# A transformer block on eight cores: the K and V projections of an attention stage moved into its layer-norm loop

## What is computed

```python
def _L1_attn_ref(x, wq, bq, wk, bk, wv, bv, wo, bo):
    q = jnp.einsum('bsd,hde->bhse', x, wq) + bq
    k = jnp.einsum('bsd,hde->bhse', x, wk) + bk
    v = jnp.einsum('bsd,hde->bhse', x, wv) + bv
    scale = 1.0 / jnp.sqrt(jnp.asarray(q.shape[-1], q.dtype))
    scores = jax.nn.softmax(jnp.einsum('bhse,bhte->bhst', q, k) * scale, axis=-1)
    att = jnp.einsum('bhst,bhte->bhse', scores, v)
    b, h, s, e = att.shape
    att = att.transpose(0, 2, 1, 3).reshape(b, s, h * e)
    return att @ wo.T + bo
```

## Time and profile before

| | us |
|---|---|
| median of the two runs | 11593.65 |
| lowest, highest | 11357.42, 11829.88 |
| the profiled execution | 11357.42 |
| its span on the slowest core | 11355.9 |
| spans of the eight cores | 11331.6 to 11355.9 |

### The profile page before, as it was taken

One profiled execution on the slowest core, in us unless ns is written; L12 is line 12 of the kernel. 1 busy time (PEld: TensorE's weight loads), 2 busy tenths in 40 slices (PEclk: granted clock), 3 DMA queues, 4 the chain that ended last, 5 costly groups with the idle time before them and its releaser, 6 DMA issues.

```text
span 11355.9 us, 101042 instructions; the slowest of 8 cores (11331.6 to 11355.9 us)
## 1 busy us (share of the span) xinstructions
PE 6804.2 (60%) x28548; PEld 2633.3 (23%) x28548; DVE 3976.3 (35%) x10242; ACT 3012.2 (27%) x6372; POOL 254.0 (2%) x410
## 2 busy tenths in 40 slices
PE   3344325545777748888833443255457777488888
PEld 2122111112222213333311221121122222133333
DVE  2443452233222232333424434522332222333334
ACT  1111123422555520111111111234225555201111
POOL 1000000001000000000000000000010000000000
PEclk7566557666888869999965665576668888699999
DMA  3000100003000011212220001000030000112121
GB/s 61 1 1 1 12 2 1 1 0 23 8 1 1 1 16 29 38 30 37 39 68 1 1 1 10 3 1 1 0 23 8 1 1 1 18 27 38 30 38 45
DMA packets 228448, 174.16 MB, mean 15 GB/s; under 512 B 137158, under 2 KB 188360, under 8 KB 227916
## 3 DMA queue, kind: packets, MB, share of 16 engines
q0 software_dynamic: 218688, 134.11, 9.0%
q1 hardware_dynamic: 9228, 33.58, 0.9%
HBM read 284.99 MB, written 16.78 MB: 27 GB/s over the span
## 4 chain that ended last, share of the span: by engine, by line
PE 46%; DVE 25%; ACT 12%; issue 11%; DMA 4%; DVEq 1%; SPq 0%; ACTq 0%; another core or an unknown queue 0%; POOL 0%; POOLq 0%
PE PS L1087 8%; PE PS L1100 5%; ACT AR L576 5%; PE PS L586 5%; DVE AR L601 4%; DVE AR L878 3%; DVE AR L1107 3%; PE PS L1040 2%; PE PS L1460 2%; PE PS L1019 2%; PE PS L844 2%; PE PS L1025 2%; PE PS L417 2%; DMA AR<-w2t 1%; PE PS L1484 1%
## 5 line engine op out<-in xcount | busy, mean ns | idle before, releaser
L576 ACT ACTIVATE AR<-PS 128x512 bf16<-128x512 f32 x2048 | 1119.3, 595 | 1166.6 <-PE PS L552 1002.1
L1107 DVE SCALAR_TENSOR_TENSOR AR<-PS,AR 128x512 f32<-128x512 f32 x1024 | 768.4, 751 | 1392.3 <-PE PS L1100 1335.4
L1087 PE MATMUL PS<-AR 128*128 128x512 bf16 x4096 | 944.1, 389 | 185.7 <-DMA AR<-w2t 185.7
L1100 PE MATMUL PS<-AR 128*128 128x512 bf16 x4096 | 988.0, 378 | 81.8 <-ACT AR L1092 25.4
L586 PE MATMUL PS<-AR 128*65 128x512 bf16 x2048 | 844.4, 428 | 202.3 <-ACT AR L576 191.6
L601 DVE RECIPROCAL AR<-PS 64x512 bf16<-64x512 f32 x128 | 428.8, 3350 | 1461.5 <-PE PS L596 1461.5
L417 PE MATMUL PS<-AR 128*128 128x128 bf16 x1024 | 210.5, 267 | 1059.3 <-DVE AR L412 925.7
L1092 ACT ACTIVATE AR<-PS 128x512 bf16<-128x512 f32 x512 | 305.8, 597 | 1859.5 <-PE PS L1087 1853.9
L1087 PEld LDWEIGHTS PS<-AR 128*128 128x128 bf16 x4096 | 404.3, 99 | 707.2 <-issue 243.7
L834 ACT ACTIVATE AR<-PS 128x512 bf16<-128x512 f32 x1024 | 523.1, 596 | 46.0 <-PE PS L812 45.2
L1100 PEld LDWEIGHTS PS<-AR 128*128 128x128 bf16 x4096 | 344.9, 96 | 704.3 <-issue 435.5
(11 more groups left out here) (229 smaller groups left out, 8285.1 us busy)
## 6 DMA issues: line engine op xcount, KB each, us to landing
AR<-w1t POOLq DMA_DIRECT2D x32, 1024.0 KB, 8.9
AR<-w2t POOLq DMA_DIRECT2D x32, 1024.0 KB, 8.8
AR<-x SPq DMA_DIRECT2D x32, 512.0 KB
y<-AR SPq DMA_DIRECT2D x32, 512.0 KB
AR<-sfc1t POOLq DMA_DIRECT2D x8, 1024.0 KB, 10.3
AR<-sfc2t POOLq DMA_DIRECT2D x8, 1024.0 KB, 15.4
AR<-sfc3t POOLq DMA_DIRECT2D x8, 1024.0 KB, 11.6
AR<-L_attn_Wq POOLq DMA_DIRECT2D x16, 256.0 KB, 13.3
```

The lines of the kernel that those rows point to most:

```text
L576: r.op("scalar", lambda s, ps=ps, pt=pt: s.activation(pt[:, 0:NIQ], ps[:, 0:NIQ], AF.Exp, bias=0.0, scale=0.125), reads=[ps.K], writes=[pt.K])
L1087: r.op("tensor", lambda t, e=e, tb=tb, hc=hc, c=c, PHx=PHx, w1T=w1T: t.matmul(PHx[:, 0:512], w1T[:, c * 512 + hc * 128: c * 512 + (hc + 1) ...
L1100: r.op("tensor", lambda t, tt=tt, dh=dh, hc=hc, PMx=PMx, hw=hw, w2T=w2T: t.matmul(PMx[:, 0:512], hw[:, hc * 512 + tt * 128: hc * 512 + tt ...
L1107: r.op("vector", lambda v, i=i, e=e, dh=dh, PMx=PMx: v.scalar_tensor_tensor(moeacc[:, i * D + dh * 512: i * D + dh * 512 + 512], PMx[:, 0: ...
```

## The change

Three edits. The two scratch tiles of the layer norm become one, in all stages. In L1 attention the call of the layer norm moves from the start of the stage to a place behind the weight issues and the bias loads. And the K and V projections become a callback of it: after each row tile's norm come the two halves of V for that tile, and after every fourth tile all eight K groups of that block of 512 rows. The V matmuls now name only the columns of `ufm` that they read. The number of matmuls, evictions and loads is the same. Since the norm now allocates behind the weights, its scratch lies above `bv_row`, in the bytes that the bias loads use for their row.

```diff
@@ emit_ln_ufm
     stats = ctx.sb(8 * nt, F32)
-    sq = [ctx.sb(D, F32), ctx.sb(D, F32)]
+    _sq = ctx.sb(D, F32)
+    sq = [_sq, _sq]
     utm = [ctx.sb(D, BF16), ctx.sb(D, BF16)]
@@ emit_l1_attn
     ufm = ctx.sb(nd * T, BF16)
-    emit_ln_ufm(ctx, R, ufm, T, D)
 
     kfm = [ctx.sb(T, BF16) for _ in range(npair)]
...
     pk = [ctx.pbank(0), ctx.pbank(1)]
-    for p in range(npair):
-        for icol in range(T // 512):
-            pp = pk[icol % 2]
...
-    for i in range(nt):
+
+    def kv_tile(i):
         for half in range(2):
             pp = pk[half % 2]
...
                     start=False, stop=(c == nd - 1)),
-                    reads=[ufm.K, wv_sb.K], writes=[pp.K])
+                    reads=[ufm.k(c * T + i * 128, c * T + (i + 1) * 128), wv_sb.K], writes=[pp.K])
...
+        if i % 4 == 3:
+            icol = i // 4
+            for p in range(npair):
+                pp = pk[p % 2]
+                for c in range(nd):
+                    r.op("tensor", lambda t, p=p, icol=icol, c=c, pp=pp: t.matmul(
+                        pp[:, 0:512], warn[p][:, c * 128:(c + 1) * 128],
+                        ufm[:, c * T + icol * 512: c * T + icol * 512 + 512],
+                        start=(c == 0), stop=(c == nd - 1)),
+                        reads=[warn[p].K, ufm.K], writes=[pp.K])
+                r.op("vector", lambda v, p=p, icol=icol, pp=pp: v.tensor_scalar(
+                    kfm[p][:, icol * 512:(icol + 1) * 512], pp[:, 0:512],
+                    bk_cols[:, p:p + 1], None, ALU.add),
+                    reads=[pp.K, bk_cols.k(p, p + 1)], writes=[kfm[p].k(icol * 512, (icol + 1) * 512)])
+
+    emit_ln_ufm(ctx, R, ufm, T, D, tile_cb=kv_tile)
     A.release()
```

## The result

| | before | after |
|---|---|---|
| median of all runs, us | 11658.27 (12 runs) | 11718.84 (13 runs) |
| lowest run, us | 11357.42 | 11531.80 |
| profiled execution, us | 11357.42 | 11543.04 |

The ratio of after to before is 1.0131, with a 95% interval of 1.0069 to 1.0193: slower, by less than the 2% that was called measurable. The profiled execution of after took 11543.0 us where 11538 was forecast. The median of all runs is 11718.84, outside the stated range of 11468 to 11595.

A forecast was written before the change was run, and what follows sets the result against it. A latency-bound norm precedes PE-bound K and V; the change makes the first V wait for loads. Stage delays of +93.9 and +86.5, together +180.4, on 11357.4 give 11538 us, 1.6% slower; range 11468 to 11595.

The forecast's parts named there:

- the wait for the loads and its queue: First V matmul waits for bo's landing, later transposes queued behind it on PE; PE idle 96 us in the first sequence.
- the chain behind V's second eviction: Next tile's small DVE operations follow V's second eviction; 5.97 us between V bursts, hiding only 2 of the norm's 7.9.
- the clock of V: Each V burst starts at 1.2 GHz and rises to 2.4 GHz within it, taking 6.2 us.
- the parts costed at nothing: One scratch tile instead of two, in all four stages, and the bf16 tiles moving down 4 KB: cost 0.
- The wq loads: Before the first Q matmul, three loads stay hidden under the last K: cost 0, else up to 4 us a sequence.
- Rival A: V stays at 1.2 GHz in all bursts, 7.69 us each: 48 us more, 11586 us, over 2% slower; chance 0.12.
- What the prediction took from Part 4 of that page: Transposes do not count as clock activity in the same way; the norm's 0.50 clock was said to agree.
- The 4.3 us at the low level: Time at 1.2 GHz within a V burst, taken as the middle of 5.5 and 2.9 us: 10 matmuls at 0.427.
- Rival B: V runs at 2.4 GHz throughout, 4.30 us a burst: 60 us less, 11477 us; chance 0.08.
- Rival C: No stall, since the weight loads start well before 2598 and land in time: 11353 us, or 11293; chance 0.05.
- D: The load chain's own length changes from 115 and 105 us: +9 or -9 us; no separate chance given.
- the base of the sum: Predicted delay added to the profiled execution, 11357.4 us, rather than the median 11593.65 of two runs 472 us apart.

The follow-up runs named there:

- e2: Changed kernel with the V/K callback for tile i called after the norm of tile i+12; ratio to before 1.0127, lowest run 11493.2 us, stage 264.8 us.
- e8: The kernel of e2 repeated in more rounds; ratio to before 1.0021, lowest run 11345.8 us, stage 265.0 and 263.5 us.
- e3: Changed kernel with wk and wv loads batched side by side; ratio to before 1.0061, lowest run 11439.8 us, stage 300.0 and 295.1 us.
- e4: Kernel before the change with the same batched wk and wv loads; ratio to before 1.0047, lowest run 11363.0 us, stage 264.7 and 263.9 us.
- e5: Changed kernel with the norm cut in two, next tile's front part ahead of V; lowest run 11601.4 us, no ratio, stage 301.2 and 304.0 us (core 5).
- e6: Changed kernel with unread matmuls added, 14 behind each V burst and three between transposes; lowest of four runs 11646.2 us, stage 322.9 us in one sequence.
- e9: The kernel of e6 repeated; ratio to before 1.0078, lowest of ten runs 11459.8 us, stage 320.7 and 318.5 us.
- e1: Kernel before with only the norm moved and one scratch tile, K and V in old order; ratio to before 0.9997, lowest run 11362.4 us.
- e7: Changed kernel with batched loads, norm cut in two and callback four tiles later; ratio to before 0.9925, lowest run 11299.1 us, stage 226.7 and 226.2 us.

## Why the prediction was right or wrong, point by point

| term, sequence 1 | forecast | after |
|---|---|---|
| tile 0 transposed at | 2617 | 2616.9 |
| idle time of PE at the first V | 96 | 92.1 |
| memset to first V | 114.7 | 111.5 |
| V burst, mean of 16 | 6.2 | 6.4 (5.6 to 7.2) |
| gap between V bursts | 5.97 | 5.6 to 6.1 |
| K, eight groups | 13.8 | 13.8 |
| first V to first Q | 244.0 | 246.7 |
| stage longer than before | +93.9 | +93.4 |

In the second sequence the first V came 108.2 us after the memset (105.5 forecast) and the first Q 247.5 later; the stage is 355.7 us, 92.7 more than before (86.5 forecast). Together +186.1 of the 185.6 by which the span grew, 11541.5 against 11355.9, so everything outside the stage stayed as it was. That the first sequence came within 0.5 us is partly luck: its load chain was 3.2 us shorter than forecast, and what follows 2.7 longer.

The mechanism is shown by the runs: the wait for the loads and its queue (e2, e8, e3, with e4 as the control), the chain behind V's second eviction (e5, less the part that is clock), the clock of V (e6, e9), and the parts costed at nothing (e1). The wq loads stayed hidden, as costed: the three that the first Q matmul needs were issued as below, while the last K groups ran until 2955.92, and the Q matmuls started at 2955.76 with no wait.

```profile
2944.38 0.93 POOL L477 DMA_DIRECT2D AR<-L_attn_wq  x1 [237.25 <-PE PS L521]
2948.53 1.75 POOL L477 DMA_DIRECT2D AR<-L_attn_wq  x2 [3.22 <-PE PS L521]
...
2955.76 1.89 PE L566 MATMUL PS<-AR 128*128 128x512 bf16 x8
```

Rival A (V at 1.2 GHz throughout) falls: the burst shown above began at 0.51 and ended at 1.00, and none of the 32 took the 7.69 us of the low level or the 4.23 of the high one. The rule of the Trainium skill's "TensorE: Matmul & The Clock Gate", section "Why this matters for your kernels", holds as far as the gaps do put the clock back; but within each burst it rose again, so the price was 2.2 us a burst and not 3.4. What the prediction took from Part 4 of that page, on transposes, is not tested by the norm's 0.50, since PE was idle for 100 of the 126.7 us there. The 4.3 us at the low level were the middle of two rows and no more; that the mean of the bursts bears them out (twice the 2.2 us lost, an estimate) is in part luck, since single bursts had about 2.7 to 6 us. Rival B falls with A. Rival C falls: the memset starts at 2597.56, after the same line's end as before. D, the length of the chain, was within its bounds (111.5 and 108.2).

What failed is the base of the sum, the step "The profiled execution took 11357.4: forecast 11538 us", with "I work against that one". The prediction took 11357.4 for the time of the kernel before, though the two runs shown lay 472 us apart, and built the range of 127 us around it, with nothing in it for the scatter of whole runs. The runs showed in its place a median of 11658.27 over 12 runs of before, 300.9 above that base, and of 11718.84 over 13 runs of after, 187.0 above its own lowest. The term added to the base was sound: +180.4 forecast, +186.1 in the stages of the two profiled executions, and 1.3% (0.7 to 1.9) in the ratio where 1.6% was forecast. With the median that it had, 11593.65, the same terms give 11774 and a range of 11704 to 11831, which holds 11718.84. That too would have been in part luck: the two medians lie only 60.6 us apart where the spans lie 185.6 apart, since the scatter added less to after than to before, and what sets the scatter is open.

Smaller misses: the chain of waits for bo came 3 us earlier in one sequence and 3 later in the other, and V's mean was 0.2 short.

## What to carry to other kernels

On an in-order queue, work that needs a slow input must not be placed ahead of work that needs none: before moving a consumer forward, look up when its last input lands, and what stands behind it in the queue. Interleaving two streams in program order overlaps them only if the order on every shared engine does too; here the norm's small DVE operations stood behind V's evictions, and only 2 of the norm's 7.9 us a tile were hidden; with the norm cut in two it was 4.5 (7.9 less a mean gap of 3.4). Where the inputs were there in time and the norm was cut (e7), the interleave did gain. Bursts with gaps between them pay for the clock as well, here 2.2 us in each.

## What the runs showed of the hardware

The sixteen wv loads of 128 KB, of which each waits for the one before, were issued 4.0 us apart in the mean in after (59.6 us for 15 steps). In e3, 32 such loads side by side took 53.6 us with two small ones, at 79 GB/s in place of 38. POOL itself paused in that batch for 7.6 and 9.9 us with no wait that the profile shows; the cause of these pauses is open.

The clock of a V burst in after fell in a gap of 5.6 to 6.1 us, of which 3.2 or more were empty and 2.7 held transposes, and rose again within the burst. In e5's first sequence, away from the K groups, the six bursts behind a gap of 2.8 us took the 4.23 us of the high level, and the six behind a gap of 4.0 us took 5.8 to 5.9. In e6, with 14 matmuls in the empty part and three between the transposes, 15 of the 16 bursts in the sequence shown took 4.23.
